# Self-attention of layer 3 on Trainium2: one unrolled block, three score buffers, whole outputs ahead of the transposes

## The chip, the cores and the metric

The kernel is one program on one core of a Trainium2 chip. The metric is the device time of one execution in microseconds (us). The engines are TensorE (PE, its weight loads PEld), VectorE (DVE), ScalarE (ACT), GpSimd (POOL) and SyncE (SP), whose queue issues the DMAs.

## The reference

A four-layer network on x of shape (2, 1024, 256). Each layer adds a gated attention and a gated feed-forward part. Layer 3's attention begins with this self-attention (a1, 16 heads of width 32), followed by an MLP, a cross-attention to 64 keys with the same widths (a2) and another MLP:

```
q = einsum('bsc,hcd->bhsd', xn, wq); k, v likewise
a = softmax(einsum('bhsd,bhtd->bhst', q, k) * D ** (-0.5), axis=-1)
a = a * (arange(t)[None, :] > arange(s)[:, None])      # a1 alone; after the softmax
o = einsum('bhst,bhtd->bhsd', a, v)
x_out = x + o @ li1_w + li1_b
h = gelu(_ln(x_out, ln3_g, ln3_b) @ li2_w + li2_b)
return x_out + h @ li3_w + li3_b
```

So the softmax runs over all 1024 keys, and the mask keeps only keys after the query: of the eight key chunks of 128, query tile `si` needs chunks `si` to 7 once the sums are known.

## The kernel before

The stages follow each other; each ends in a barrier. The change touches three.

**Projection** (`stage_self_project`, lines 2028 to 2186). Eight pairs of token tiles. Each pair's q and k are split into three bf16 parts and sent to DRAM (line 2070), its values too (line 2078). The first four pairs also send a second copy, into entry number 8, that nothing but a superfluous load reads. After the fourth pair SP waits for all sends and issues the 17 DMAs that load entry 0 (`load_entry`, lines 2015 to 2025); ScalarE may overwrite a buffer of parts only once its sends have landed.

**Self-attention** (`stage_self_attention`, lines 2196 to 2401). An entry is a batch and four heads, so 8 entries. An entry has 32 units: a unit is a query tile of 128 rows and one head. The tiles come in the order 0, 7, 1, 6, 2, 5, 3, 4, four heads each. A unit `v` goes through these steps:

- `scores(v)` (2292, PE): four bf16 matmuls of 512 columns into two PSUM banks. There are two such pairs of banks (0 to 3), so `scores(v)` waits for the exponential of unit v-2.
- the row maximum (2390, DVE), the exponential with its row sum (2373, ACT), the reciprocal of the sum (2397, DVE).
- the multiplication by the reciprocal, over the columns from `si * 128` on (2273, POOL, `tensor_tensor` with a broadcast operand), and the mask on the diagonal chunk (2276, POOL).
- `turn(v)` (2308, PE, five units later): 8 - si transposes, in one or two bankfuls (two where more than four chunks), banks 4 and 5 in turn; the even bankful is copied out by ACT (2359), the odd by DVE (2361).
- `output(w, q)` (2326, PE): w is a group of four units (a tile). From ten units later on, its matmuls of 32 columns (four heads at four column positions of the array) run in four visits q, one per unit, each with the chunks whose number has remainder q. Banks 6 and 7; ACT copies the result out (708 by `copy_bank`).

PE's queue has per unit: scores(v), turn(v-5), a visit of output. DVE's has maximum(v), its copy of unit v-5, reciprocal(v-1). ACT's has its copy of unit v-5, exponential(v), and every fourth unit the copy of an output. Four entries form the body of a hardware loop that runs twice; at its end everything drains, the semaphores are cleared, and the next body begins with no unit in flight.

**Cross-attention** (`stage_attention`, lines 336 to 677) serves l0a (width 64), l2a (16) and l3a (32), 16 heads each. In the wide form the output weights are folded with the values beforehand (`fold_v`, line 482, four of eight folds of a chunk), and each token tile needs eight matmuls of 256 columns (542). The narrow form makes the heads' outputs first (522, from a block `v_blk` with zeros), copies them with ACT (708) and multiplies by `wo` (533). Before a turn of the norm (222) PE waits in the narrow form for that copy:

```
                    if i >= TURN and (i - TURN) % 2 == 0:
                        if narrow:
                            pe.wait_ge(heads_stored, min(i - HEADS_OUT + 1, TILES))
```

Of the kernel before, what the change touches and what calls it, by code (L numbers as in the profile page):

```python
# [15 lines left out]
B = 2  # L16
# [319 lines left out]
def stage_attention(core, a, name, width, scale, plan, following, source, out_tile, gate, bias,  # L336
# [16 lines left out]
    narrow = width * 4 <= KEYS  # L353
# [1617 lines left out]
def self_attention_scratch(nc):  # L1971


    def dram(name, shape, dtype):
        return nc.dram_tensor(name, shape, dtype, kind="Internal").ap()


    parts = [[dram(f"l3_{kind}_part{m}", [ENTRIES + 1, P, TOK], BF16) for m in range(3)] for kind in ("q", "k")]
    values = dram("l3_values", [ENTRIES + 1, P, KC, P], F32)
    heads_out = dram("l3_heads_out", [ENTRIES, P, TOK], F32)  # L1980
    return parts, values, heads_out
# [46 lines left out]
def stage_self_project(core, a, x1, scratch, entry, plan):  # L2028
# [6 lines left out]
    with ExitStack() as ctx:  # L2035
# [21 lines left out]
        with nc.Block() as block:  # L2057
            @block.sync
            def _(sp):
                total = [0, 0]  # L2060
                for k in range(PAIRS):
                    b, p, at = k // (PAIRS // B), k % 2, (k % (PAIRS // B)) * PAIR
                    places = [(b * GROUPS, GROUPS)]
                    if b == 0:
                        places.append((ENTRIES, 1))
# [23 lines left out]
            def sent_before(k):  # L2089

                return sum(16 * 8 * (2 if q < PAIRS // B else 1) for q in range(k % 2, k, 2))
# [104 lines left out]
def stage_self_attention(core, scratch, entry, following):  # L2196
# [8 lines left out]
    BODY = 4  # L2205
    RING = 8
    TURN = 5
    STORE = TURN
# [17 lines left out]
    assert BANKFULS % 2 == 0  # L2226

    def groups_through(u):

        return sum(1 for g in groups if g[0] <= u)  # L2230

    with ExitStack() as ctx:
# [13 lines left out]
        with nc.Fori(0, ENTRIES // BODY) as jj:  # L2246
            sem, clear_semaphores = named_semaphores(nc, "l3s")
            scores_ready, measured, exped, inverted = sem("scores_ready"), sem("measured"), sem("exped"), sem("inverted")
            masked, turned, stored = sem("masked"), sem("turned"), [sem("stored0"), sem("stored1")]
            out_ready, out_stored = sem("out_ready"), sem("out_stored")  # L2250
            out_sent = [sem(f"out_sent{e}") for e in range(BODY)]

            with nc.Block() as block:
                @block.sync
                def _(sp):
                    load_entry(sp, scratch, entry, BODY * jj + 1, 1)
                    for e in range(BODY):

                        sp.wait_ge(out_ready, KC * (e + 1))
                        if e < BODY - 1:  # L2260
                            load_entry(sp, scratch, entry, BODY * jj + e + 2, e % 2)
                        sp.wait_ge(out_stored, KC * (e + 1))
                        sp.dma_start(out_scratch[bass.ds(BODY * jj + e, 1)].rearrange("a p n -> p (a n)"),
                                     heads_out[:, e % 2, :]).then_inc(out_sent[e], 16)
                    for e in range(BODY):
                        sp.wait_ge(out_sent[e], 16)

                @block.gpsimd
                def _(pool):
                    for v in range(BODY * UNITS):  # L2270
                        si = tile_of(v)
                        pool.wait_ge(inverted, v + 1)
                        nc.gpsimd.tensor_tensor(ex[v % RING][:, si * P:], ex[v % RING][:, si * P:],  # L2273
                                                sm[:, v % RING:v % RING + 1].to_broadcast([P, TOK - si * P]), ALU.mult)
                        pool.drain()
                        nc.gpsimd.affine_select(out=ex[v % RING][:, si * P:(si + 1) * P], in_=ex[v % RING][:, si * P:(si + 1) * P],
                                                compare_op=ALU.is_gt, fill=0.0, base=0, pattern=[[1, P]],
                                                channel_multiplier=-1).then_inc(masked, 1)
# [449 lines left out]
```

## Time and profile before

| | us |
|---|---|
| median of 3 runs (2547.37 to 2549.26) | 2548.7 |
| the profiled execution | 2524.31 |
| its span | 2522.6 |
| projection's last pair to self-attention's first matmul | 951 to 967.0 |
| self-attention, first body | 967.0 to 1225.9 |
| self-attention, second body, to its last DMA | 1225.9 to 1477.1 |
| first l3a fold to the next stage's first matmul | 1666.7 to 1831.6 |

Mean granted clock of PE over the span 0.902 of full speed. An engine's busy time is what its instructions take; back to back they can overlap by some 0.1 us, so starts are the better measure of pace.

### The profile page before, as it was taken

The numbers are of one execution on the slowest core, as the hardware profiler recorded it, in microseconds if no ns is written. First come the engines' busy times: TensorE is split into PE (matmuls) and PEld (weight loads), VectorE is DVE, ScalarE is ACT, GpSimd is POOL, SyncE is SP. The second block draws the span as 40 slices with busy tenths as digits, with TensorE's granted clock in tenths as the row PEclk, the third lists the DMA queues.
The fourth block names the chain that finished last, engine by engine and source line by source line (L and its number), as shares of the span: only waits on it lengthen the run. The fifth ranks groups of instructions, "written<-read, shape, count | busy, mean of one in ns | idle before, by whom it ended". The sixth has DMA issues, their size and how long they took to land. (4 is left out here: it accounts for less than half of the span.)

```text
span 2522.6 us, 36317 instructions
## 1 busy us (share of the span) xinstructions
PE 2047.2 (81%) x11904; PEld 1504.7 (60%) x11904; DVE 1367.6 (54%) x3511; ACT 929.6 (37%) x1859; POOL 710.5 (28%) x1199
## 2 busy tenths in 40 slices
PE   5983974467867677999799979969898589999991
PEld 4661863354444454555455558846687378888991
DVE  4871006535745765888688847757636432222332
ACT  4220321112324346888688843232232112222230
POOL 0223011030130125777577751102330230000005
PEclk9995995578979789999999989979999699999995
DMA  2004531000011286333333430110000525555684
GB/s 87 1 1 150 167 104 28 13 13 14 1 19 12 82 216 165 85 85 85 86 65 92 97 108 11 28 36 1 1 13 1 193 104 175 175 175 175 215 287 115
DMA packets 171504, 219.20 MB, mean 87 GB/s; under 512 B 39911, under 2 KB 133540, under 8 KB 165184
## 3 DMA queue, kind: packets, MB, share of 16 engines
q1 hardware_dynamic: 163344, 196.65, 26.7%
q0 software_dynamic: 7264, 20.31, 2.5%
q8 instruction: 88, 1.44, 0.2%
q14 instruction: 88, 0.72, 0.1%
q10 hardware_dynamic: 720, 0.07, 0.0%
HBM read 171.13 MB, written 46.14 MB: 86 GB/s over the span
## 5 line engine op out<-in xcount | busy, mean ns | idle before, releaser
L2390 DVE TENSOR_REDUCE l3s_mx<-banks 128x1 f32<-128x1024 f32 x256 | 313.1, 1223 | 96.7 <-PE banks L2292 93.8
L2292 PE MATMUL banks<-l_stack 128*128 128x512 bf16 x1024 | 268.1, 385 | 44.1 <-ACT xn_tokens L2373 21.0
L1012 PE MATMUL banks<-l3f_xrt,l3f_w 128*128 128x256 f32 (+1 forms) x1536 | 277.9, 342 | 2.7 <-issue 1.5
L1012 PEld LDWEIGHTS banks<-l3f_xrt,l3f_w 128*128 128x128 f32 x1536 | 249.6, 192 | 29.1 <-issue 3.3
L1302 DVE TENSOR_SCALAR l3f_sg<-banks 128x256 f32<-128x256 f32 (+1 forms) x192 | 72.0, 375 | 287.5 <-PE banks L1012 287.5
L2273 POOL TENSOR_TENSOR xn_tokens<-xn_tokens,l3s_sm 128x1024 f32<-128x1024 f32 (+3 forms) x128 | 201.6, 1575 | 50.3 <-DVE l3s_sm L2397 49.2
L222 PE MATMUL banks<-ident,xn_tokens 128*128 128x128 f32 x320 | 64.7, 338 | 166.8 <-DVE xn_tokens L211 148.0
L2292 PEld LDWEIGHTS banks<-l_stack 128*128 128x128 bf16 x1024 | 80.8, 98 | 163.3 <-ACT xn_tokens L2373 52.6
L2373 ACT ACTIVATE xn_tokens<-banks,l3s_mx 128x1024 f32<-128x1024 f32 x128 | 142.7, 1115 | 46.2 <-DVE l3s_mx L2390 45.1
L222 PEld LDWEIGHTS banks<-ident,xn_tokens 128*128 128x128 f32 x320 | 46.6, 172 | 188.4 <-DVE xn_tokens L211 133.0
L2373 ACT ACTIVATE x_features<-banks,l3s_mx 128x1024 f32<-128x1024 f32 x128 | 143.0, 1117 | 27.9 <-DVE l3s_mx L2390 27.6
L1077 ACT ACTIVATE l3f_sg<-l3f_sg 128x256 f32<-128x256 f32 (+1 forms) x192 | 72.2, 376 | 208.9 <-DVE l3f_sg L1302 208.9
L1025 PE MATMUL banks<-l3f_w,l3f_ht 128*128 128x256 f32 x624 | 138.5, 379 | 0.0
L930 POOL DMA_DIRECT2D l3f_results<-l3f_yt x24 | 15.8, 658 | 410.7 <-ACT l3f_yt L708 410.7
L1025 PEld LDWEIGHTS banks<-l3f_w,l3f_ht 128*128 128x128 f32 x624 | 116.8, 190 | 14.9
L2537 PE MATMUL banks<-x_features,weights 128*128 128x256 f32 x512 | 117.5, 390 | 4.3 <-ACT x_features L235 2.4
L2308 PEld LDWEIGHTS banks<-ident,xn_tokens 128*128 128x128 f32 x832 | 96.5, 140 | 29.1 <-issue 10.2
L2550 PE MATMUL banks<-weights,l3m_ht 128*128 128x256 f32 x512 | 113.2, 379 | 0.4 <-DVE l_x L2605 0.4
L2308 PE MATMUL banks<-ident,xn_tokens 128*128 128x128 f32 x832 | 112.6, 273 | 0.5 <-ACT l3s_pt L2359 0.5
L2537 PEld LDWEIGHTS banks<-x_features,weights 128*128 128x128 f32 x512 | 100.1, 196 | 19.5 <-issue 3.8
L2273 POOL TENSOR_TENSOR x_features<-x_features,l3s_sm 128x128 f32<-128x128 f32 (+3 forms) x128 | 92.4, 722 | 65.6 <-DVE l3s_sm L2397 64.6
L2359 ACT ACTIVATE l3s_pt<-banks 128x384 f32<-128x384 f32 (+2 forms) x192 | 97.0, 505 | 24.2 <-PE banks L2326 18.5
(532 smaller groups left out, 3925.4 us busy)
## 6 DMA issues: line engine op xcount, KB each, us to landing
l3f_w<-in_L_ffn_gate_up_w_dram SPq DMA_DIRECT2D x24, 2048.0 KB, 7.6
l3f_w<-in_L_ffn_down_w_dram SPq DMA_DIRECT2D x24, 1024.0 KB, 6.0
l_stack<-l_q_part SPq DMA_DIRECT2D x72, 256.0 KB, 6.0
l_stack<-l_k_part SPq DMA_DIRECT2D x72, 256.0 KB, 11.4
l0f_w<-in_L_ffn_W_dram SPq DMA_DIRECT2D x16, 1024.0 KB, 5.8
l_q_part<-l_stack SPq DMA_DIRECT2D x24, 256.0 KB, 3.0
l_k_part<-l_stack SPq DMA_DIRECT2D x24, 256.0 KB, 3.7
l3f_rows<-l3f_zero SPq DMA_DIRECT2D x13, 384.0 KB, 4.1
```

Of the source, the lines that this page charges most:

```text
L222: last = nc.tensor.transpose(ps[:, bank, c * PAIR + u * P:c * PAIR + (u + 1) * P], src(2 * j + u)[:, c * P:(c + 1) * P], core["ident"][:, :])
L1012: last = nc.tensor.matmul(ps[:, f % 4, h * PAIR:h * PAIR + size], w1_sb[:, p, dc, h * FF + f * P:h * FF + (f + 1) * P], xrt[:, p, dc, 0:si ...
L1025: last = nc.tensor.matmul(ps[:, 4 + p, u * D:(u + 1) * D], ht[:, p, f, u * P:(u + 1) * P], w2_sb[:, p, f, :], start=(f == 0), stop=(f == F ...
L1077: nc.scalar.activation(sg[:, f % 4, 0:size], sg[:, f % 4, 0:size], ACT.Silu).then_inc(silued, 1)
L2273: nc.gpsimd.tensor_tensor(ex[v % RING][:, si * P:], ex[v % RING][:, si * P:], sm[:, v % RING:v % RING + 1].to_broadcast([P, TOK - si * P]) ...
L2292: last = nc.tensor.matmul(ps[:, 2 * (v % 2) + h, :], stack[p][0][s][:, r, si * P:(si + 1) * P], stack[p][1][s][:, r, h * 512:(h + 1) * 512 ...
L2308: last = nc.tensor.transpose(ps[:, 4 + n % 2, c * P:(c + 1) * P], ex[v % RING][:, (si + c0 + c) * P:(si + c0 + c + 1) * P], core["ident"][ ...
L2359: last = op.activation(dst, src, ACT.Copy)
L2373: nc.scalar.activation(ex[v % RING][:, :], ps[:, 2 * (v % 2):2 * (v % 2) + 2, :].rearrange("p a n -> p (a n)"), ACT.Exp, bias=mx[:, v % RI ...
L2390: nc.vector.tensor_reduce(mx[:, v % RING:v % RING + 1], ps[:, 2 * (v % 2):2 * (v % 2) + 2, :].rearrange("p a n -> p (a n)"), AX_X, ALU.max ...
L2537: last = nc.tensor.matmul(ps[:, n % 4, 0:PAIR], w2[:, dc, f * P:(f + 1) * P], core["xt"][:, dc, PAIR * j:PAIR * (j + 1)], start=(dc == 0), ...
L2550: last = nc.tensor.matmul(ps[:, 4 + k % ring, u * D:(u + 1) * D], ht[:, k % 2, f, u * P:(u + 1) * P], w3[:, f, :], start=(f == 0), stop=(f ...
```

## The change

One entry after the other in a single block of 8 entries, unrolled (before, a loop of two bodies). The score buffers are three pairs of banks (0 to 5). Transposes and outputs share banks 6 and 7 in the order of their use (`uses`), and whoever empties a bank is given by the parity of the use: ACT even, DVE odd. By that rule the outputs fall to DVE (w = 0 to 63, all odd), and of an entry's 48 bankfuls of transposes 28 go to ACT and 20 to DVE.

```diff
-    narrow = width * 4 <= KEYS
+    narrow = width * 2 <= KEYS
...
-    parts = [[dram(f"l3_{kind}_part{m}", [ENTRIES + 1, P, TOK], BF16) for m in range(3)] for kind in ("q", "k")]
+    parts = [[dram(f"l3_{kind}_part{m}", [ENTRIES, P, TOK], BF16) for m in range(3)] for kind in ("q", "k")]
...
-                    if b == 0:
-                        places.append((ENTRIES, 1))
...
+    SCORES = 3
+
+    uses, last_turn = {}, {}
+    for v in range(ENTRIES * UNITS + OUT):
+        if v >= OUT and (v - OUT) % R == 0:
+            uses["out", (v - OUT) // R] = len(uses)
+        if TURN <= v < ENTRIES * UNITS + TURN:
+            for g, group in enumerate(groups):
+                if group[0] == (v - TURN) % UNITS:
+                    uses["turn", (v - TURN) // UNITS, g] = len(uses)
+                    last_turn[(v - TURN) // R] = uses["turn", (v - TURN) // UNITS, g]
...
-        with nc.Fori(0, ENTRIES // BODY) as jj:
...
-                        nc.gpsimd.tensor_tensor(ex[v % RING][:, si * P:], ex[v % RING][:, si * P:],
-                                                sm[:, v % RING:v % RING + 1].to_broadcast([P, TOK - si * P]), ALU.mult)
+                    nc.gpsimd.tensor_scalar(ex[v % RING][:, si * P:], ex[v % RING][:, si * P:],
+                                            sm[:, v % RING:v % RING + 1], None, ALU.mult)
...
+                    if v >= SCORES:
+                        pe.wait_ge(exped, v - SCORES + 1)
...
+                def output(w):
+                    e, si = w // KC, ORDER[w % KC]
+                    n = uses["out", w]
+                    for side in range(2):
+                        pe.wait_ge(stored[side], stored_through(side, max(last_turn[w], n - 2 if side == n % 2 else 0)))
+                    for c in range(si, KC):
+                        for r in range(R):
+                            last = nc.tensor.matmul(ps[r * W:(r + 1) * W, 6 + n % 2, 0:P],
+                                                    values[:, e % 2, c, r * W:(r + 1) * W],
+                                                    pt[:, w % 2, r, c - si, :], start=(c == si),
+                                                    stop=(c == KC - 1))
+                    last.then_inc(out_ready, 1)
...
+                    if v < ENTRIES * UNITS:
+                        scores(v)
+                    if v >= OUT and (v - OUT) % R == 0:
+                        output((v - OUT) // R)
+                    if TURN <= v < ENTRIES * UNITS + TURN:
+                        turn(v - TURN)
...
+            @block.scalar
+            def _(act):
+                for v in range(ENTRIES * UNITS + OUT + 1):
+                    store_output(act, nc.scalar, v, 0)
+                    if v >= TURN:
+                        store_turned(act, nc.scalar, v - TURN, 0)
...
+            @block.vector
+            def _(dve):
+                for v in range(ENTRIES * UNITS + OUT + 1):
+                    store_output(dve, nc.vector, v - 1, 1)
+                    if v >= TURN + 1:
+                        store_turned(dve, nc.vector, v - TURN - 1, 1)
+                    if v < ENTRIES * UNITS:
+                        dve.wait_ge(scores_ready, v + 1)
...
```

`stored_through(side, n)` counts the uses of a side up to n. So DVE's queue has output(v-1) and its copy of unit v-6 ahead of maximum(v), then reciprocal(v-1). `narrow` now holds for width 32 too, so l3a takes the narrow form.

## Rows read from the trace of the kernel before

**Rows 1.** The page: busy time of each engine, share of the span, instructions.

```profile
PE 2047.2 (81%) x11904; PEld 1504.7 (60%) x11904; DVE 1367.6 (54%) x3511; ACT 929.6 (37%) x1859; POOL 710.5 (28%) x1199
```

**Rows 2.** Windows, self-attention: length, then busy us (instructions) by engine, clock.

```profile
967.00:1225.90 258.90, 237.58 (x2240) 134.59 (x2241) 207.67 (x352) 200.61 (x386) 182.90 (x256) 0.99 0.37 87
...
1046.80:1107.60 60.80, 58.59 (x560) 33.41 (x558) 51.57 (x89) 49.68 (x96) 45.47 (x64) 1.00 0.38 88
```

**Rows 3.** Timeline of SP's queue: the load that follows each entry's last output.

```profile
1046.86 3.64 SPq L2023 DMA_DIRECT2D l_stack<-l_q_part  x8
...
1108.02 4.19 SPq L2023 DMA_DIRECT2D l_stack<-l_q_part  x8
```

**Rows 4.** Timeline of PE: start us, modelled us, line, instructions in a run.

```profile
1057.69 0.93 PE L2308 MATMUL banks<-ident,xn_tokens 128*128 128x128 f32 x7
1058.45 1.03 PE L2292 MATMUL banks<-l_stack 128*128 128x512 bf16 x4
...
1080.30 0.64 PE L2326 MATMUL banks<-l3s_pt,l_values_in 128*32 128x128 f32 x16
...
1101.87 1.04 PE L2292 MATMUL banks<-l_stack 128*128 128x512 bf16 x4
1102.75 1.04 PE L2308 MATMUL banks<-ident,xn_tokens 128*128 128x128 f32 x8
1103.71 0.43 PE L2326 MATMUL banks<-l3s_pt,l_values_in 128*32 128x128 f32 x8
1104.07 1.04 PE L2292 MATMUL banks<-l_stack 128*128 128x512 bf16 x4
```

**Rows 5.** Waits, 1010 to 1190 us: total us, times, longest.

```profile
PE banks L2292 <- ACT xn_tokens L2373: 5.8, 15, 0.6
```

**Rows 6.** Timeline of PE: the first scores of the second loop body.

```profile
1225.90 3.59 PE L2292 MATMUL banks<-l_stack 128*128 128x512 bf16 x8 [8.15 <-issue]
```

**Rows 7.** Groups by shape, 1010 to 1190 us.

```profile
L2390 DVE TENSOR_REDUCE l3s_mx<-banks 128x1 f32<-128x1024 f32 x95 | 116.2, 1223 | 26.5 <-PE banks L2292 25.2
...
L2373 ACT ACTIVATE xn_tokens<-banks,l3s_mx 128x1024 f32<-128x1024 f32 x48 | 53.5, 1115 | 15.2 <-DVE l3s_mx L2390 14.8
...
L2273 POOL TENSOR_TENSOR xn_tokens<-xn_tokens,l3s_sm 128x1024 f32<-128x1024 f32 x12 | 22.7, 1895 | 0.2
...
L2361 DVE COPY l3s_pt<-banks 128x384 f32<-128x384 f32 x29 | 15.9, 548 | 0.6 <-PE banks L2326 0.6
...
L2397 DVE RECIPROCAL l3s_sm<-l3s_sm 128x1 f32<-128x1 f32 x94 | 14.3, 153 | 0.0
...
L2273 POOL TENSOR_TENSOR x_features<-x_features,l3s_sm 128x128 f32<-128x128 f32 x12 | 4.8, 401 | 8.7 <-DVE l3s_sm L2397 8.5
...
L2361 DVE COPY l3s_pt<-banks 128x128 f32<-128x128 f32 x6 | 1.7, 280 | 0.0
```

**Rows 8.** Timeline of the projection stage: SP's queue and ScalarE.

```profile
906.70 2.17 SPq L2070 DMA_DIRECT2D l_q_part<-l_stack  x3
...
914.27 3.68 SPq L2023 DMA_DIRECT2D l_stack<-l_q_part  x8
...
942.92 1.09 ACT L2139 ACTIVATE l_stack<-banks 128x512 bf16<-128x512 f32 x2 [9.00 <-DMA l_values<-l3p_vs]
```

**Rows 9.** Windows of line 482 alone, folds of layer 3's cross-attention.

```profile
1670.00:1682.00 12.00, 11.44 (x53) 9.63 (x52) 1.00 0.01 1
```

**Rows 10.** Timeline of PE in layer 3's cross-attention (l3a).

```profile
1734.56 3.62 PE L542 MATMUL banks<-l3a_fold_v,l3a_pt 128*128 128x256 f32 x16
```

**Rows 11.** Timeline of PE in layer 2's cross-attention (l2a), the narrow form.

```profile
680.77 0.64 PE L522 MATMUL banks<-l2a_pt,l2a_v_blk 128*32 128x128 f32 x16
681.34 1.13 PE L533 MATMUL banks<-l2a_wo,l2a_heads 128*128 128x256 f32 x4
...
685.13 0.66 PE L222 MATMUL banks<-ident,xn_tokens 128*128 128x128 f32 x4 [2.66 <-ACT l2a_heads L708]
...
701.25 4.83 PE L499 MATMUL banks<-l2a_fold_q,x_features 128*128 128x512 f32 x8
```

More of the change, by code:

```diff
@@ L2089, in sent_before @@
             def sent_before(k):
-                return sum(16 * 8 * (2 if q < PAIRS // B else 1) for q in range(k % 2, k, 2))
+                return sum(16 * 8 for q in range(k % 2, k, 2))
             @block.gpsimd
@@ L2349, in store_turned @@
                     for g, (u, c0, size) in enumerate(groups):
[L2350 to L2351 removed]
+                        if u != v % UNITS:
                             continue
[L2353 to L2357 removed]
@@ L2399, in stage_self_attention @@
-            clear_semaphores()
-        nc.sync.wait_ge(loaded[0], 16 * LOADS * (ENTRIES // 2 + 1))
-        nc.all_engine_barrier()
+                        n = uses["turn", e, g]
+                        if n >= 2:
+                            pe.wait_ge(stored[n % 2], stored_through(n % 2, n - 2))
+                        for c in range(size):
+                            last = nc.tensor.transpose(ps[:, 6 + n % 2, c * P:(c + 1) * P],
+                                                       ex[v % RING][:, (si + c0 + c) * P:(si + c0 + c + 1) * P],
+                                                       core["ident"][:, :])
@@ new lines, in _ @@
+                for v in range(ENTRIES * UNITS + OUT):
+                    if v < ENTRIES * UNITS and v % UNITS == 0:
+                        e = v // UNITS
+                        pe.wait_ge(loaded[e % 2], 16 * LOADS * (e // 2 + 1))
+                    if v < ENTRIES * UNITS:
[4 more added lines that the diff above has]
+                        turn(v - TURN)
@@ new lines, in store_turned @@
+            def store_turned(eng, op, v, side):
+                if v >= ENTRIES * UNITS:
+                    return
+                e, w = v // UNITS, v // R
+                for g, (u, c0, size) in enumerate(groups):
+                    if u != v % UNITS or uses["turn", e, g] % 2 != side:
+                        continue
+                    n = BANKFULS * e + g
+                    eng.wait_ge(turned, n + 1)
+                    if w >= 2:
+                        eng.wait_ge(out_ready, w - 1)
+                    dst = pt[:, w % 2, v % R, c0:c0 + size, :].rearrange("p c n -> p (c n)")
+                    src = ps[:, 6 + side, 0:size * P]
+                    if side == 0:
+                        last = op.activation(dst, src, ACT.Copy)
+                    else:
+                        last = op.tensor_copy(dst, src)
+                    last.then_inc(stored[side], 1)
@@ new lines, in store_output @@
+            def store_output(eng, op, v, side):
+                if not OUT <= v < ENTRIES * UNITS + OUT or (v - OUT) % R != 0:
+                    return
+                w = (v - OUT) // R
+                e, si = w // KC, ORDER[w % KC]
+                if uses["out", w] % 2 != side:
+                    return
+                eng.wait_ge(out_ready, w + 1)
+                if e >= 2:
+                    eng.wait_ge(out_sent[e % 2], 16 * (e // 2))
+                dst, src = heads_out[:, e % 2, si * P:(si + 1) * P], ps[:, 6 + side, 0:P]
+                last = op.activation(dst, src, ACT.Copy) if side == 0 else op.tensor_copy(dst, src)
+                last.then_inc(stored[side], 1)
@@ L2404, in self_out_weights @@
+        clear_semaphores()
 def self_out_weights(a):
```

201 lines of the change are left out of this document (62 added, 139 removed).

## The prediction

> **What bounds the kernel now.** The page first: PE is busy 81% of the span, DVE 54% [rows 1], an average over stages; the change lies in three of them, so I read those. The windows of self-attention come next: its first body takes 258.9 us, and in a steady stretch of 60.8 us PE is busy 58.59, DVE 51.57, ACT 49.68, POOL 45.47, at granted clock 1.00 [rows 2]. SP's queue gives the exact pace: the load behind an entry's last output starts at 1046.86 and at 1108.02, so **an entry takes 61.16 us** (the next ones 61.1 too) [rows 3]. Eight would take 489; the stage takes 510 because of its loop.
>
> Then PE's timeline, for what a unit costs PE by starts. Scores: 0.88 (1101.87 to 1102.75). A transpose: 0.109 (seven in 0.76). Eight of them before an output: 0.96, so up to 0.09 more at that change. An output visit of 8 records (one chunk, four heads) 0.36 (1103.71 to 1104.07); 16 records take 0.64 modelled where 8 take 0.43: 0.21 a chunk and 0.15 for the visit itself [rows 4]. An entry has 32 units, 4 x 36 = 144 transposes, 36 chunks and, by the remainders q, 4+1+4+2+4+3+4+4 = 26 visits. PE's own time is 32 x 0.88 + 144 x 0.109 + 36 x 0.21 + 26 x 0.23 (0.15 and 0.08 of the change) = 28.2 + 15.7 + 7.6 + 6.0 = 57.5 us. Measured 61.1: **3.6 us an entry are waits**. The list of waits has PE idle before scores for the exponential 5.8 us in 180 [rows 5], 2.0 an entry; the rest is gaps too short to be listed. So PE is the bound, with two score buffers as the second.
>
> **The parts.**
>
> *The loop.* The second body's first scores start at 1225.90 after 8.15 us idle [rows 6]; fill and drain around it cost too. All of it: 258.9 - 4 x 61.1 = **14.5 us** [rows 2, 3]. Unrolled, the join goes: minus 14.5. Only an instruction stream twice as long stands against that; it is fetched in either form, and I cost it at nothing.
>
> *Outputs whole.* 26 visits become 8: 18 x 0.23 = 4.1 us of PE an entry (18 x 0.15 = 2.7 if the change between shapes costs nothing). Chunks and matmuls stay. PE's own time becomes 53.4.
>
> *Three score buffers.* Scores wait for the exponential of v-3. The 3.6 us of waits can go, but they can't become a gain to the full, since other waits come up.
>
> *One pair of banks for transposes and outputs.* All outputs are DVE's, and it takes them behind the maximum and the reciprocal. After an output of tiles 7, 6, 5 or 4 come units with two bankfuls; the first goes to ACT's bank, the second needs the bank of the output. DVE has it free, counted from the end of scores(v), after the maximum 1.22, a reciprocal 0.15, the copy of 128 columns 0.28 [rows 7] and 0.15 that I assume for the hand-over: about 1.8. PE gets there after the output (0.36 to 1.0) and up to four transposes (0.44): 0.8 to 1.5. So stalls of 0.3 to 1.0, four an entry: **+2.4 us**.
>
> *DVE a turn later.* Its order becomes maximum(v), reciprocal(v-1), copy of v-5. Before, the copy lay between the maximum and the reciprocal, which covered the exponential of v-1 (1.12 [rows 7] and the read of its sum). Queued behind the reciprocal are now the copy, and behind that PE's next second bankful. DVE's work per entry is 51.6 us busy [rows 2]; four fewer copies (0.28 for one chunk, 0.55 for three) and eight outputs of 0.28 leave it at about 52, by starts (0.1 overlap each) about 50. In the tiles with two bankfuls a unit costs it 1.12 + 0.1 + 0.45 to 0.6 = 1.7 to 1.8 by starts, as much as PE's 0.88 + 0.87. There the two engines are even, and losses of handshake stay: I take 0.8 us an entry (0 to 3.2: sixteen units by 0.2).
>
> *GpSimd.* 1024 columns take 1895 ns, 128 take 401 [rows 7]: 1.67 ns a column. A per-partition scalar on a wide tile is not in the trace. Below, it saves nothing, since the list of waits has no wait of PE for POOL; above, see the rivals. I take 0: five units of lag cover it, and POOL has 15 us of slack an entry [rows 2]. If it were slower, `turn` would be late next.
>
> Sum for an entry: 53.4 + 2.4 + 0.8 = **56.6**, 4.5 less than 61.1; eight entries: **minus 36**. Ends: 53.4 (minus 62) and 61.1 (nothing).
>
> *Projection.* The second copies are 8 of 16 DMAs in each of four pairs. In three pairs they end long before the pair (15 us) does, and cost nothing. In the fourth SP issues six from 906.70, 3.6 us, and two of the values', 1.1, before the load of entry 0 can start at 914.27. That load fills the DMA engines, the next sends land late, and ACT waits 9.00 us at 942.92 for them [rows 8]; DVE and PE wait on ACT, to the end of the stage. 4.7 us earlier in, as much off that wait: **minus 4.5** (0 to 6).
>
> *Cross-attention l3a in narrow form.* Setup: 53 records are 26.5 folds in 12 us [rows 9], 0.45 each; 16 go, minus 7.2, and half of the first block's masking, minus 0.8. New ahead of the loop: two matmuls of 512 columns for the values (2 x 0.86 by the pace of the scores), their masking (0.7 as a 512-column copy) and hand-overs: plus 3. Net minus 5. Per tile: 8 matmuls of 256 columns take 3.62 modelled [rows 10], some 3.45 by starts, and so do the scores, 4 of 512. In their place heads and `wo`. l2a's heads, 16 records at 32 columns, take 0.57 [rows 11], against 1.75 for 16 records of 128 columns one after the other [rows 4]: four lie side by side. At 64 columns two fit: 0.14 + 0.87 = 1.0 (0.57 to 1.9). `wo` is half of the old product, 1.7, plus 0.1. So 2.8, and 0.1 for the change of shape: 0.55 less a tile. But before each norm turn PE waits for the heads' copy. In l2a it idles 2.66 and goes on at 685.13; 3.45 + 0.96 + 0.57 lie before 681.34, so that is 8.8 us after the scores began [rows 11]. l3a's PE arrives at 3.45 + 0.96 + 2.8 = 7.2, the copy of twice the columns ends at 9.0: 1.8 us idle, then 0.43 of norm. Before, such a tile took 3.45 + 0.87 + 3.45 + 0.43 = 8.2: plus 1.2. Five such turns, plus 6; eleven or so others at minus 0.55, minus 5, and a drain one turn longer, plus 3. Stage: minus 5 + 6 - 5 + 3 = minus 1; with what the clock may take (below) I book **plus 1** (-6 to +14).
>
> Of the clock: after the idle in l2a, the scores at 701.25 took 4.83 modelled us [rows 11], as many columns at the full clock 3.62 [rows 10], that is, part of them ran at 1.2 GHz instead of 2.4. The Trainium skill, TensorE: Matmul & The Clock Gate, section "A second HAM failure mode: psum-queue depth-cycling", says that short idles between groups of matmuls while cycling through PSUM banks are enough to make the clock fall and rise. By that rule self-attention, which cycles through banks all the time, should swing, and it is granted 1.00 [rows 2]: the measurement decides there.
>
> Total: -14.5 - 36 - 4.5 + 1 = -54. The profiled execution took 2524.31, so it would be 2470; it lay 24.4 below the median of the runs shown, and against that the **forecast is 2548.7 - 54 = 2495 us**.
>
> **The rivals.**
> - *DVE ties PE* (23%). The second bankful of a unit needs DVE's copy of the unit before, so PE can't run ahead however many score buffers there are, and the third does not do what it says. For it: 16 units an entry with two bankfuls, each 0.2 later. Against: by starts DVE has 10 us of slack an entry. Price: 56.6 + 2.9 = 59.5 an entry, minus 13; total minus 31: 2518.
> - *PE at its floor* (17%). The stalls fall where PE is ahead and cost nothing: 53.4 to 54.5 an entry, minus 57; total minus 75: 2474.
> - *The clock falls in l3a* (5%). PE idles 1.8 us ahead of five turns and again in the drain; at 1.2 GHz scores take 1.2 more in each as at 701.25, and heads and `wo` after the drain's idles twice their 2.8. Five by 1.2 and three by 2.8 are plus 14: 2509. That is the page's rule taken to this stage.
> - *GpSimd becomes the bound* (5%, the side slower than before). Place: the multiplication by a per-partition scalar. An entry has 18432 columns; at 1.67 ns 31 us, and 15 for the rest of POOL with 6 of gaps. It decides from 63 us an entry, or 2.3 ns a column. At twice today's 1.67: 21 + 62 = 83, eight times 22 more, less 18 gained elsewhere: 2707. Against: it reads one wide operand where `tensor_tensor` reads two. The Trainium skill, GPSIMD Engine Reference, section 3.1, gives 1.8 cycles an element as the best of a one-input loop and 2.6 for two inputs; no run here shows the first, and the second disagrees with rows 7 (1.67 ns are 2.0 cycles at the page's 1.2 GHz).
> - *Nothing gained beyond the join* (3%): new stalls eat the visits saved, l3a costs what the rest gives: within 0.2%.
>
> **How the numbers follow.** The forecast's own case (2480 to 2508) has 47%. Faster by over 0.2% (5 us, about what a measurement of this kernel can tell): all but the last two cases, 0.92; same 0.03; slower 0.05. The range takes in the floor's upper part and most of the DVE case: 2467 to 2528; it leaves out the GpSimd case and the ends of both.
>
> **What would show it.** The stage from first scores to last output near 455 us, one entry per 56.6 by SP's loads; no idle of 8 us in its middle; 8 output runs an entry; waits of the transposes (2308's line) for DVE near 2.4 us an entry; hardly any of scores for the exponential. ACT's wait near 942.92 at about 4.5. GpSimd's rows at or under 1895 ns. l3a: 16 folds fewer, heads of about 1.0, `wo` of 1.8, idle before norm turns near 1.8. It would be wrong if entries stay near 60, if the transposes wait for POOL, or if l3a's loop grows by more than 10.

## The result, and the profile of the changed kernel

The changed kernel takes **2583.3 us** (median of 4 runs, 2580.0 to 2586.0) where the kernel before takes 2548.0 on the same chip (2546.3 to 2549.3): ratio 1.0147, interval 1.0131 to 1.0163. That is 35 us slower; forecast were 54 us faster, and a range that ends at 2528. The profiled execution took 2580.03, its span 2578.4 us.

The page first, the busy time of each engine, and two of its groups, both of GpSimd's multiplication.

```profile
PE 2019.7 (78%) x11996; PEld 1498.2 (58%) x11996; DVE 1370.9 (53%) x3538; ACT 925.8 (36%) x1826; POOL 854.6 (33%) x1202
...
L2282 POOL TENSOR_SCALAR xn_tokens<-xn_tokens,l3s_sm 128x1024 f32<-128x1024 f32 (+3 forms) x128 | 302.5, 2363 | 15.1 <-DVE l3s_sm L2403 15.1
...
L2282 POOL TENSOR_SCALAR x_features<-x_features,l3s_sm 128x128 f32<-128x128 f32 (+3 forms) x128 | 138.6, 1083 | 0.1
```

Against [rows 1] PE, DVE and ACT hardly differ; POOL has 144 us more to do. Its column of idle says what that means: it waited 15.1 us for a row sum, once, at the start, and never again. An engine that waits for nobody is the one that others wait for. The windows of one steady entry and of the stage, against [rows 2]:

```profile
1043.70:1112.10 68.40, 57.34 (x560) 34.89 (x560) 52.56 (x93) 49.32 (x92) 63.84 (x65) 1.00 0.33 78
964.00:1518.60 554.60, 463.29 (x4480) 281.11 (x4480) 421.34 (x736) 396.23 (x737) 511.38 (x512) 0.99 0.30 69
```

POOL (the last of the five busy times) is busy 63.84 of 68.40 us, and the rest are its own short gaps. SP's queue gives the entry, as in [rows 3]:

```profile
1043.64 4.59 SPq L2023 DMA_DIRECT2D l_stack<-l_q_part  x8
...
1112.10 3.65 SPq L2023 DMA_DIRECT2D l_stack<-l_q_part  x8
...
1180.27 3.64 SPq L2023 DMA_DIRECT2D l_stack<-l_q_part  x8
```

**68.3 us an entry**, where 61.1 were and 56.6 were forecast. The groups by shape, 1010 to 1190 us, give the cause; the same instructions of [rows 7] took 1895 ns for 1024 columns and 401 for 128:

```profile
L2282 POOL TENSOR_SCALAR xn_tokens<-xn_tokens,l3s_sm 128x1024 f32<-128x1024 f32 x12 | 34.1, 2843 | 0.0
...
L2285 POOL TENSOR_SCALAR_AFFINE_SELECT x_features<-x_features 128x128 f32<-128x128 f32 x43 | 12.6, 293 | 6.0 <-issue 0.4
...
L2282 POOL TENSOR_SCALAR x_features<-x_features,l3s_sm 128x128 f32<-128x128 f32 x12 | 7.2, 603 | 0.0
```

(2843 - 603) / 896 columns is **2.50 ns a column**, where `tensor_tensor` took 1.67, and 0.28 us are left for the instruction itself (0.19 before). An entry's 18432 columns and 32 instructions are 46.1 + 9.1 = 55.2 us, the 32 selections 9.4, the gaps ahead of them 4.4: 69, within 1 us of the entry measured. The waits of 1010 to 1190 us (total, times, longest) name POOL, which in [rows 5] stood nowhere:

```profile
PE banks L2313 <- POOL xn_tokens L2285: 22.0, 23, 1.7
PE banks L2325 <- DVE l3s_pt L2359: 3.5, 7, 0.7
PE banks L2313 <- POOL x_features L2285: 2.3, 6, 0.4
```

Last the ends of the stages in PE's timeline: last output of self-attention and start of l3a in the kernel before, then in the changed kernel first scores, last output, start of l3a and start of the stage behind it; and ScalarE's wait in the projection, against [rows 8]:

```profile
1475.57 1.08 PE L2326 MATMUL banks<-l3s_pt,l_values_in 128*32 128x128 f32 x32 [0.26 <-issue]
...
1660.87 1.94 PE L462 MATMUL banks<-ident,weights 128*128 128x128 f32 x8 [1.97 <-PEq L44]
```

```profile
964.09 7.43 PE L2297 MATMUL banks<-l_stack 128*128 128x512 bf16 x20 [11.99 <-PEq L44]
...
1516.70 1.08 PE L2325 MATMUL banks<-l3s_pt,l_values_in 128*32 128x128 f32 x32 [0.69 <-ACT l3s_pt L2357]
...
1699.61 1.94 PE L462 MATMUL banks<-ident,weights 128*128 128x128 f32 x8 [1.96 <-PEq L44]
...
1864.81 15.54 PE L2541 MATMUL banks<-x_features,weights 128*128 128x256 f32 x64 [1.97 <-PEq L44]
```

```profile
940.06 1.08 ACT L2137 ACTIVATE l_stack<-banks 128x512 bf16<-128x512 f32 x2 [6.02 <-DMA l_values<-l3p_vs]
```

Self-attention begins at 964.09 (967.00 before: 2.9 earlier) and its last output starts 552.6 us later, where before it was 508.6: plus 44.0. The MLP behind it takes 182.9 against 185.3, l3a (1699.61 to 1864.81) 165.2 against 170.7. In all -2.9 + 44.0 - 2.4 - 5.5 = **+33 of the 35 us**. The experts' stage behind (layer 3's feed-forward) took 713.6 us in this trace and 691.0 in that of before (an execution of 2524.31); the medians, taken on one chip, leave hardly room for a difference there, and the experiments below are compared either with before on their own chip or stage by stage up to the experts.

### The profile page after: what moved, and what is told of

It is laid out like the page before. It is cut to its first block and busy times, and to the rows that moved or that the text cites. A ratio compares the mean times of both kernels' runs of the same rounds, so it can differ in the third digit from the quotient of the medians.

```text
span 2578.4 us, 36316 instructions
## 1 busy us (share of the span) xinstructions
PE 2019.7 (78%) x11996; PEld 1498.2 (58%) x11996; DVE 1370.9 (53%) x3538; ACT 925.8 (36%) x1826; POOL 854.6 (33%) x1202
## 5 line engine op out<-in xcount | busy, mean ns | idle before, releaser
L2282 POOL TENSOR_SCALAR xn_tokens<-xn_tokens,l3s_sm 128x1024 f32<-128x1024 f32 (+3 forms) x128 | 302.5, 2363 | 15.1 <-DVE l3s_sm L2403 15.1
L222 PE MATMUL banks<-ident,xn_tokens 128*128 128x128 f32 x320 | 65.0, 339 | 173.0 <-DVE xn_tokens L211 147.4
L2313 PE MATMUL banks<-ident,xn_tokens 128*128 128x128 f32 x832 | 125.9, 282 | 68.1 <-POOL xn_tokens L2285 59.9
L2313 PEld LDWEIGHTS banks<-ident,xn_tokens 128*128 128x128 f32 x832 | 89.3, 140 | 123.9 <-POOL xn_tokens L2285 98.9
L222 PEld LDWEIGHTS banks<-ident,xn_tokens 128*128 128x128 f32 x320 | 46.1, 172 | 196.4 <-DVE xn_tokens L211 125.7
L930 POOL DMA_DIRECT2D l3f_results<-l3f_yt x24 | 15.7, 656 | 435.0 <-ACT l3f_yt L708 435.0
L2357 ACT ACTIVATE l3s_pt<-banks 128x384 f32<-128x384 f32 (+3 forms) x224 | 109.3, 488 | 114.2 <-PE banks L2313 113.6
L2297 PEld LDWEIGHTS banks<-l_stack 128*128 128x128 bf16 x1024 | 101.3, 99 | 81.9 <-issue 16.4
L2282 POOL TENSOR_SCALAR x_features<-x_features,l3s_sm 128x128 f32<-128x128 f32 (+3 forms) x128 | 138.6, 1083 | 0.1
L2359 DVE COPY l3s_pt<-banks 128x384 f32<-128x384 f32 (+3 forms) x160 | 88.1, 551 | 54.4 <-PE banks L2313 53.3
```

The costliest lines, as they stand in the source:

```text
L222: last = nc.tensor.transpose(ps[:, bank, c * PAIR + u * P:c * PAIR + (u + 1) * P], src(2 * j + u)[:, c * P:(c + 1) * P], core["ident"][:, :])
L2282: nc.gpsimd.tensor_scalar(ex[v % RING][:, si * P:], ex[v % RING][:, si * P:], sm[:, v % RING:v % RING + 1], None, ALU.mult)
L2297: last = nc.tensor.matmul(ps[:, 2 * (v % SCORES) + h, :], stack[p][0][s][:, r, si * P:(si + 1) * P], stack[p][1][s][:, r, h * 512:(h + 1) ...
L2313: last = nc.tensor.transpose(ps[:, 6 + n % 2, c * P:(c + 1) * P], ex[v % RING][:, (si + c0 + c) * P:(si + c0 + c + 1) * P], core["ident"][ ...
L2357: last = op.activation(dst, src, ACT.Copy)
L2359: last = op.tensor_copy(dst, src)
```

## The experiments

The theory after the result: GpSimd's `tensor_scalar` costs 2.50 ns a column and bounds the stage; the rest of the change is a gain. Rivals: the unrolled order with two shared banks made the stage slow and GpSimd only shows it; or the gain expected of the rest isn't there either.

### 1. The old multiplication in the changed kernel (e1_tensor_tensor)

```diff
-nc.gpsimd.tensor_scalar(ex..., ex..., sm[:, v % RING:v % RING + 1], None, ALU.mult)
+nc.gpsimd.tensor_tensor(ex..., ex..., sm[:, v % RING:v % RING + 1].to_broadcast([P, TOK - si * P]), ALU.mult)
```

> The changed kernel with GpSimd's multiplication in the old form (tensor_tensor with a broadcast operand). Theory, GpSimd is the bound: its rows return to 1895 ns at 1024 columns, an entry falls from 68.2 us to about 56.6, eight of them 93 less, total near 2490. Rival, the two shared banks and VectorE's late emptying hold the stage nearly as much: an entry stays at 60 or more, total 2518 or more, and transposes then wait for VectorE by over 4 us an entry.

**2488.6 us where before takes 2520.2**: ratio 0.9873 (0.9854 to 0.9892). The ratios 1.0147 and 0.9873 differ by 2.7%, some 69 us, and that is GpSimd's line (by the traces its stage takes 487.1 us in place of 552.6, 65.5 less); the rows of 1024 columns are back at 1893 ns. But the rest gains 31.5 us and not 54. The total near 2490 that the first theory named was met by luck: it counted from before's 2548, and on this chip before takes 2520. SP's loads:

```profile
1093.85 3.65 SPq L2023 DMA_DIRECT2D l_stack<-l_q_part  x8
...
1335.48 3.81 SPq L2023 DMA_DIRECT2D l_stack<-l_q_part  x8
```

Four entries in 241.63 us: **60.4 an entry**, 0.7 under before and not 4.5, as the rival had it (60 or more). PE's timeline shows where the time is, around an output of tile 7:

```profile
1104.98 0.60 PE L2313 MATMUL banks<-ident,xn_tokens 128*128 128x128 f32 x4
1105.92 0.55 PE L2313 MATMUL banks<-ident,xn_tokens 128*128 128x128 f32 x3 [0.34 <-ACT l3s_pt L2357]
...
1108.04 0.43 PE L2325 MATMUL banks<-l3s_pt,l_values_in 128*32 128x128 f32 x8 [0.71 <-DVE l3s_pt L2359]
1108.39 0.66 PE L2313 MATMUL banks<-ident,xn_tokens 128*128 128x128 f32 x4
1109.34 0.55 PE L2313 MATMUL banks<-ident,xn_tokens 128*128 128x128 f32 x3 [0.29 <-DVE weights L2374]
```

Three waits belong to one output: 0.34 ahead of it, 0.71 for the bank that it shares with a bankful not yet copied, 0.29 for the copy of the output itself. I had booked only the last, at 2.4 us an entry. Over the entry from 1214.74 it takes 0.5 (the rival expected over 4), the first 0.9, and the wait of outputs for VectorE's copy, booked at nothing, 2.7. Summed by starts over one entry, each step to the start of the next less the idle shown in brackets (before: 1108.02 to 1169.11; this kernel: 1214.74 to 1274.86):

| us an entry | forecast took, before | trace, before | forecast, after | trace, this kernel |
|---|---|---|---|---|
| scores | 28.2 | 28.1 | 28.2 | 27.4 (28.9) |
| transposes | 15.7 | 18.9 | 15.7 | 19.7 (18.2) |
| outputs | 13.6 | 12.0 | 9.5 | 9.0 |
| idle listed | 3.6 | 2.1 | 3.2 | 4.1 |
| sum | 61.1 | 61.1 | 56.6 | 60.1 |

In this trace 8 of an entry's 128 records of scores are missing, and their time stands under transposes. How much that is, two traces of one kernel show, those of experiment 10: 27.4 and 19.5 us with 120 records, 29.0 and 18.0 with 128. The numbers in brackets are this kernel's with 1.5 us put back; experiment 8, at the same pace with all 128 records, reads 28.9 and 18.2. The transposes are the row that matters: 144 x 0.109 leaves out 3.2 us in before and 2.5 here, by the likeliest reading what each short run of them costs beside its columns, which no run took apart. In before the outputs, booked 1.6 too high, hid half of it: of the 3.6 us that I called waits only 2.1 were. Those did go, since nothing of scores for the exponential is listed here; 4.1 of waits for banks came in their place.

### 2. The new multiplication in the kernel before

```diff
-nc.gpsimd.tensor_tensor(ex..., ex..., sm[...].to_broadcast([P, TOK - si * P]), ALU.mult)
+nc.gpsimd.tensor_scalar(ex..., ex..., sm[...], None, ALU.mult)
```

> The kernel before with only GpSimd's multiplication in the new form. Theory, GpSimd is the bound: 2.5 ns a column make GpSimd 68 us an entry whatever the order of the rest, so an entry takes 68 instead of 61.1: plus 56 us, total near 2604. Rival, the long instruction is hidden by five units of lag, and it is the new order that exposes it: total within 10 us of 2548.

2583.2 against 2520.2: ratio **1.0244** (1.0227 to 1.0261), 63 us. Entries go to 68.3 (1124.49 to 1192.75), the same as in the changed kernel, whatever the order of the work:

```profile
1124.49 4.34 SPq L2023 DMA_DIRECT2D l_stack<-l_q_part  x8
...
1192.75 3.66 SPq L2023 DMA_DIRECT2D l_stack<-l_q_part  x8
```

```profile
L2273 POOL TENSOR_SCALAR xn_tokens<-xn_tokens,l3s_sm 128x1024 f32<-128x1024 f32 x9 | 25.6, 2844 | 0.0
```

Eight entries by 7.2 us are 58. Most of the other 5 lie where a body fills: from the load at its start to the next, 968.98 to 1056.27 and 1253.80 to 1346.40, it takes 9.4 us more than in before (968.92 to 1046.86, 1222.54 to 1305.76), 2.2 above the 7.2, twice. The one line alone makes either kernel slow.

### 3. An immediate in place of the pointer

```diff
-nc.gpsimd.tensor_scalar(ex..., ex..., sm[:, v % RING:v % RING + 1], None, ALU.mult)
+nc.gpsimd.tensor_scalar(ex..., ex..., 0.001, None, ALU.mult)
```

> The changed kernel with GpSimd's multiplication by an immediate (0.001) in place of the per-partition scalar: the division by the row sums is left out and all weights are scaled by a constant, the shape and count of the instructions stay. If the pointer to a per-partition scalar is what costs 2.50 ns a column, the immediate runs at 1.67 ns a column or less: 1024 columns take 1.9 us or less, an entry falls from 68.4 us to about 60.5, and the run ends some 60 us below the changed kernel, near 2490 us where before takes 2520. If tensor_scalar itself runs at 3 cycles of 1.2 GHz a column on this engine, the 1024 columns stay at 2.84 us, the entries at 68 us and the run near 2550.

This kernel leaves out the division by the row sums. It ran once: 2534.5 us, where before takes 2522.1. The groups by shape, 1050 to 1430 us:

```profile
L2282 POOL TENSOR_SCALAR xn_tokens<-xn_tokens 128x1024 f32<-128x1024 f32 x21 | 58.1, 2769 | 0.0
...
L2282 POOL TENSOR_SCALAR x_features<-x_features 128x128 f32<-128x128 f32 x21 | 11.1, 529 | 0.0
```

(2769 - 529) / 896 is 2.50 ns a column again. The per-partition pointer costs 74 ns an instruction and nothing a column: it is `tensor_scalar` itself that goes at this pace here, and the second theory holds for the columns. Its entries of 68 us and total near 2550 came out lower, since I had not expected the 74 ns: entries by SP's loads are 65.6 (1106.23 to 1368.43 for four), 2.7 fewer, of which 32 x 0.074 = 2.4 are the instructions.

### 4. Two score buffers

```diff
-    SCORES = 3
+    SCORES = 2
```

on the kernel of experiment 1.

> The first experiment with two score buffers instead of three. If the third buffer carries a part of the gain, an entry grows by the 2 to 3.6 us of waits that the kernel before had: plus 16 to 29 us on the first experiment. Rival, VectorE's emptying ties TensorE so closely that the third buffer is never used: within 5 us of the first experiment.

2540.4 against 2520.2: ratio 1.0081 (1.0062 to 1.0100), **52 us more than with three**. Both numbers that I gave were too small.

```profile
1108.30 3.64 SPq L2023 DMA_DIRECT2D l_stack<-l_q_part  x8
...
1174.35 4.28 SPq L2023 DMA_DIRECT2D l_stack<-l_q_part  x8
```

```profile
POOL x_features L2282 <- DVE l3s_sm L2403: 35.7, 36, 2.1
DVE l3s_mx L2398 <- PE banks L2297: 35.3, 74, 1.1
...
PE banks L2297 <- ACT xn_tokens L2387: 19.6, 41, 0.8
```

An entry takes 66.05. POOL waits for row sums, VectorE for scores (35.7 and 35.3 us in 240), and PE before scores for the exponential: 6.2 us over the entry from 1108.30, where with three buffers none is listed and in before 2.1. So the third buffer is worth 5.6 us an entry in this order, and the new order with its shared banks costs about 5 by itself. The likely mechanism, argued and not shown: PE, held for a bank, comes late with scores, and with two buffers nothing is in hand. The two parts belong together, and what the forecast counted as two gains is one that pays for the other.

### 5. l3a in its wide form

```diff
-    narrow = width * 2 <= KEYS
+    narrow = width * 4 <= KEYS
```

on the kernel of experiment 1.

> The first experiment with layer 3's cross-attention in the wide form of before. From the traces of before and after that stage takes 170.7 and 165.2 us, so this should be 5.5 us slower than the first experiment (3 to 8). Rival, the stage's gain is given back by the next one's start: within 2 us.

2497.3: ratio 0.9905 (0.9889 to 0.9922), **8.6 us more**, just over the 3 to 8 expected, and the traces give l3a 173.3 us in place of 165.0. The narrow form is worth 5.5 (changed against before) to 8.6 us.

### 6. The projection's second copies sent again

```diff
                     places = [(b * GROUPS, GROUPS)]
+                    if b == 0:
+                        places.append((ENTRIES, 1))
```

with the scratch and the counts as before, on the kernel of experiment 1.

> The kernel of e1_tensor_tensor, with the projection's second copies of entry 0 sent again (8 of 16 DMAs in four pairs). The forecast's step says 4.5 us slower than e1 (0 to 6); the two profiled executions of before and after differ by 2.9 at the start of the stage. If SP's queue ahead of entry 0's load is not what ends ScalarE's wait, within 1 us of e1.

2521.1 where before takes 2544.7 on that chip: ratio 0.9905 (0.9890 to 0.9920). Against experiment 1's ratio that would be 8 us, but chips differ behind self-attention; the traces up to there are cleaner. The load of entry 0 starts at 914.36 (910.53 in experiment 1), the longest of ScalarE's waits is 8.1 (5.3), self-attention begins at 965.84 (962.78), 3.1 us later. But 0.9 of it was there before the stage: the projection's first matmul starts at 841.35 and 840.42. From that matmul on, entry 0's load comes 73.0 to 73.1 us later in all three traces with the second copies (this one, before, experiment 2) and 70.0 to 70.1 later in the others, and self-attention begins 124.5 to 126.2 us later in the three and 121.8 to 123.4 in the eleven traces without them: **2.9 us** by the means, the load's 2.9 to 3.0. From its first scores to its last output the stage takes 486.7 and 487.1, the same.

```profile
914.36 3.66 SPq L2023 DMA_DIRECT2D l_stack<-l_q_part  x8
...
965.84 5.67 PE L2299 MATMUL banks<-l_stack 128*128 128x512 bf16 x16 [11.66 <-PEq L44]
```

```profile
ACT l_stack L2139 <- DMA l_values<-l3p_vs: 9.5, 2, 8.1
```

### 7. VectorE's copies at their old place (e6_vector_early)

```diff
-                    store_output(dve, nc.vector, v - 1, 1)
-                    if v >= TURN + 1:
-                        store_turned(dve, nc.vector, v - TURN - 1, 1)
...
+                    store_output(dve, nc.vector, v, 1)
+                    if v >= TURN:
+                        store_turned(dve, nc.vector, v - TURN, 1)
```

ahead of the reciprocal, on the kernel of experiment 1.

> The kernel of e1_tensor_tensor, with VectorE's copies of turned tiles and of outputs back behind the maximum of the same turn, as in the kernel before. If the later turn was needed, VectorE now waits for transposes that stand behind scores and an output in TensorE's queue, its reciprocals and next maximum come late, and entries go from 60.5 us to 61 to 62: 4 to 12 us slower than e1 (2493 to 2501 where before takes 2520). If instead the copy ahead of the maximum is what holds maximum, exponential and scores up, entries fall to 59 to 60 us: 4 to 12 us faster than e1. If VectorE has slack at both places, within 3 us of e1.

2484.1 against 2522.1: ratio **0.9846** (0.9829 to 0.9862). The interval touches that of experiment 1; the traces settle it: 59.1 us an entry (four in 236.41), 1.3 fewer, 480.1 for the stage where 487.1 were. The same output as above:

```profile
1106.88 0.43 PE L2325 MATMUL banks<-l3s_pt,l_values_in 128*32 128x128 f32 x8 [0.45 <-DVE l3s_pt L2359]
...
1108.18 0.55 PE L2313 MATMUL banks<-ident,xn_tokens 128*128 128x128 f32 x3 [0.29 <-DVE weights L2374]
```

0.45 in place of 0.71 for the bank. "A turn later" was a loss: over an entry these waits fall from 2.7 us to 1.7, and whatever VectorE's early copy delays in its own queue costs less than its late one costs PE.

### 8. Only VectorE's copy of an output earlier

```diff
-                    store_output(dve, nc.vector, v - 1, 1)
...
+                    store_output(dve, nc.vector, v, 1)
```

> The kernel of e1_tensor_tensor, with only VectorE's copy of an output (half of the 64) moved from ahead of the next turn's maximum to behind its own turn's maximum; turned tiles are still emptied a turn later. If the waits for banks end the time (0.29 us behind an output before the transposes that need its bank), 32 of these go, some 5 to 9 us faster than e1. If the entry is set by the chain of maximum, exponential and scores, the reciprocal comes a little later and the run stays within 3 us of e1.

2488.7: ratio 0.9868 (0.9850 to 0.9887), no difference from experiment 1 that can be told; 60.1 us an entry. All the outputs are VectorE's, not half of them as I wrote there, and moving these copies alone gains at most 0.3 an entry: the copies of turned tiles are what most of experiment 7's gain comes from.

### 9. Outputs behind the transposes

```diff
-                    if v >= OUT and (v - OUT) % R == 0:
-                        output((v - OUT) // R)
                     if TURN <= v < ENTRIES * UNITS + TURN:
                         turn(v - TURN)
+                    if v >= OUT and (v - OUT) % R == 0:
+                        output((v - OUT) // R)
```

with banks and copies numbered in that order, on the kernel of experiment 1.

> The kernel of e1_tensor_tensor, with outputs issued behind the transposes of their turn, banks numbered in that order. If issuing them ahead matters, each of the 64 outputs now waits for the copy of a bankful turned just before it, 0.5 to 1 us in place of the 0.6 to 0.73 us seen now for the copy of the last one: up to 1 us each, and 8 to 40 us over the stage. If the output pays one copy of a bank wherever it stands, because outputs share the two banks with the transposes, the run is within 5 us of e1.

2510.3 against 2522.1: ratio 0.9956 (0.9939 to 0.9972), **some 21 us more**; four entries take 250.83, 62.7 each.

```profile
1111.64 0.96 PE L2313 MATMUL banks<-ident,xn_tokens 128*128 128x128 f32 x7 [0.70 <-DVE l3s_pt L2359]
1113.43 0.43 PE L2325 MATMUL banks<-l3s_pt,l_values_in 128*32 128x128 f32 x8 [0.83 <-DVE l3s_pt L2359]
```

Transposes and output now wait, 0.70 and 0.83. So in this kernel, where they share banks, the output is better issued ahead.

### 10. ScalarE copies the outputs (e10_scalar_copies_outputs)

```diff
-                    store_output(act, nc.scalar, v, 0)
+                    for side in range(2):
+                        store_output(act, nc.scalar, v, side)
```

VectorE's call is gone, the bank's own semaphore is counted up as before, on the kernel of experiment 7.

> The kernel of e6_vector_early, with all outputs copied by ScalarE; until now all 64 fall to VectorE, 0.29 us each. If the shared pair of banks and VectorE's turn order set what is left above TensorE's own work (0.29 us of idle behind four outputs an entry, 2.3 us of VectorE's time an entry), entries fall from 59.7 to about 58.5 us: 6 to 12 us faster than e6, near 2475 where before takes 2520. If ScalarE's exponentials then come late (it waits for the output ahead of each one), the gain is eaten: within 3 us of e6 or slower.

2499.0 against 2544.7: ratio **0.9816** (0.9796 to 0.9837). Entries 58.6 us (four in 234.56). Run again beside the next experiment:

> The kernel of e10_scalar_copies_outputs once more, on the same chip as the run with copies chosen by place, as the measure for it: entries of 58.6 us, and 46 us less than before.

2478.9 against 2523.0, ratio 0.9826 (0.9812 to 0.9839), entries 58.6, 44 us less than before. Against experiment 7 that is 0.5 us an entry, 4 in all (5 to 8 by the ratios, taken on different chips), under the 6 to 12 expected. The wait of 0.29 behind an output is gone from the list; what is left at it:

```profile
1105.33 0.55 PE L2313 MATMUL banks<-ident,xn_tokens 128*128 128x128 f32 x3 [0.34 <-ACT l3s_pt L2357]
...
1107.19 0.43 PE L2325 MATMUL banks<-l3s_pt,l_values_in 128*32 128x128 f32 x8 [0.45 <-DVE l3s_pt L2359]
1107.55 1.20 PE L2313 MATMUL banks<-ident,xn_tokens 128*128 128x128 f32 x7
```

### 11. The engine of a copy by its place in the unit

```diff
-                    if u != v % UNITS or uses["turn", e, g] % 2 != side:
+                    bank = uses["turn", e, g] % 2
+                    pair = [q for q in range(BANKFULS) if groups[q][0] == u]
+                    if u != v % UNITS or (bank if len(pair) == 1 else pair.index(g)) != side:
```

on the kernel of experiment 10.

> The kernel of e10_scalar_copies_outputs, with the engine of a copy chosen by its place and no longer by its bank: where a unit has two bankfuls ScalarE copies the first and VectorE the second. An output then waits for a copy of ScalarE that runs during the maximum, not for one of VectorE behind it. If these waits (0.42 us, four an entry) and the 0.34 behind each change of parity are what is left, entries fall from 58.6 to 56.5 to 57.5 us: 9 to 17 us faster than e10. If the first bankful behind an output now waits for VectorE's copy of the second one before it, the wait only moves: within 4 us of e10.

2476.8 against 2523.0: ratio **0.9819** (0.9806 to 0.9832), entries 58.6: the same as experiment 10 within its interval. The wait only moved, as the second case has it:

```profile
1104.14 0.55 PE L2313 MATMUL banks<-ident,xn_tokens 128*128 128x128 f32 x3 [0.34 <-ACT l3s_pt L2359]
...
1105.94 0.43 PE L2325 MATMUL banks<-l3s_pt,l_values_in 128*32 128x128 f32 x8 [0.39 <-ACT l3s_pt L2359]
...
1107.12 0.55 PE L2313 MATMUL banks<-ident,xn_tokens 128*128 128x128 f32 x3 [0.16 <-ACT weights L2376]
```

Now ScalarE holds the output 0.39. Every one of these kernels with `tensor_tensor` in it but experiment 4's beats both kernels of the change; the best two are 1.8% under before.

## Why the prediction was wrong

**GpSimd: the step that failed.** I wrote "I take 0" for an operation that the trace of before doesn't show. It cost 2.50 ns a column where 1.67 were, and experiments 1 and 2 put 69 and 63 us on that line alone. The rival's own sum was sound: with the measured 2.50 it gives 21 + 46 = 67 an entry and, eight times 6 more less 18, some 2579; measured 2583. (The forecast with 68.3 in place of 56.6 comes to 2495 + 8 x 11.7 = 2589; the 6 between are l3a's, below.) What was wrong is its chance, 5%, its price at a doubling, and its threshold: 63 us or 2.3 ns is where the whole change becomes a loss, but by the same terms (21 beside the columns) GpSimd bounds the forecast's 56.6 from 1.93 ns a column on, 1.16 times the 1.67. The 15 us of slack were counted without its gaps and against the old, longer entry, and nothing in any row said that the unseen form could not be a sixth slower. I let "it reads one wide operand where `tensor_tensor` reads two" stand as a reason against, and the range left the case out. The Trainium skill, GPSIMD Engine Reference, section 3.1, points the same way: its best loop takes 1.8 cycles an element (one input, as I read it), and `tensor_tensor` with its two inputs 2.6. By that page the line would have become faster; at the page's 1.2 GHz the rows are 3.0 cycles for the one input and 2.0 for two. The order is the reverse, and the measurement decides.

**The steady entry.** Without GpSimd the entry is 60.4 (experiment 1), forecast 56.6. Two terms of the sum: the transposes, 15.7 booked and 18.9 in the same trace of before, which I could have found by summing one entry by starts as in the table of experiment 1; and the banks, 2.4 and 0.8 booked, 4.1 listed. Against the forecast's 56.6 experiment 1 has 2.5 more in transposes, 0.9 more in idle, 0.7 more in scores and 0.5 less in outputs. Outputs whole were worth 3.0 (4.1 forecast). What held is the rival "DVE ties PE" in its price, 59.5 an entry and 2518 in all: 0.9873 of 2548.7 is 2516. That the totals agree so well is luck: its entries are 0.9 us short (7 in all), and its l3a 7 too long. In its mechanism it held only half: it was the copy's place in VectorE's order (experiment 7 took 1.3 off) and its having every output (experiment 10 took 0.5 more), not VectorE's load. That the third buffer "does not do what it says" was wrong: experiment 4 puts 52 us on it.

**The loop.** Minus 14.5 forecast. Stage less eight entries: 508.6 - 8 x 61.1 = 19.8 before, 487.1 - 8 x 60.4 = 3.9 in experiment 1: minus 16. It held, and the longer stream of instructions shows no cost.

**The projection.** Minus 4.5 forecast, 2.9 measured (experiment 6), by the mechanism named: counted from the stage's first matmul, SP reached entry 0's load 2.9 to 3.0 earlier, and ScalarE's longest wait shrank from 9.0 and 8.1 to between 5.2 and 6.3. The size was off: I took the removed sends' 4.7 us of issuing as the shift.

**Layer 3's cross-attention.** Plus 1 forecast, minus 5.5 to 8.6 measured. Heads of 16 records take 1.03 by starts (1.0 forecast), `wo` 1.84 (1.8), idle before the norm's transposes 1.50 once and 1.28 four times (1.8). Scores stay at 3.60 modelled, where l2a's took 4.83 [rows 11]: the clock granted from 1733 to 1833 us is 1.00, so these idles did not bring it down. In the drain it did fall: the mean of the two levels, 1.2 and 2.4 GHz, is 0.78 of full speed from 1833.0 to 1864.8, where PE idles 2.78, 1.20 and 6.81 us at a time, and the heads take 1.97 modelled in place of 1.09. Before's drain has 0.88 (1797.5 to 1831.6). The tile's prices held. The lines of a steady tile, a norm turn, and last the heads and `wo` in the drain at the lower clock:

```profile
1758.27 3.60 PE L499 MATMUL banks<-l3a_fold_q,x_features 128*128 128x512 f32 x8
1761.70 1.04 PE L509 MATMUL banks<-ident,l3a_ex 128*128 128x128 f32 x8
1762.66 1.09 PE L522 MATMUL banks<-l3a_pt,l3a_v_blk 128*64 128x128 f32 x16
1763.69 1.99 PE L533 MATMUL banks<-weights,l3a_heads 128*128 128x256 f32 x8
1767.18 0.65 PE L222 MATMUL banks<-ident,xn_tokens 128*128 128x128 f32 x4 [1.50 <-ACT l3a_heads L708]
...
1846.99 1.97 PE L522 MATMUL banks<-l3a_pt,l3a_v_blk 128*64 128x128 f32 x16 [1.20 <-ACT x_features L235]
1848.89 2.90 PE L533 MATMUL banks<-weights,l3a_heads 128*128 128x256 f32 x8
```

Taken apart by PE's starts, changed kernel against before, then experiment 1 against experiment 5: the setup (to the first scores) gives -5.7 and -7.0 where -5 was forecast; from the first to the last scores -2.9 and -2.0, forecast +1; from there to the next stage +3.1 and +0.7, forecast +3 and 2 for the clock. So setup and drain were near, and the loop and the clock were priced too high. In the loop, a steady tile gains 0.51 and a norm turn loses 1.00, as forecast within 0.2; the rest lies in its first turns, up to the first `wo`, where one run of before's scores also took 5.24 modelled us in place of 3.60.

Added up for experiment 1: -16 - 8 x 0.7 - 2.9 - 5.7, and -1.8 in the MLP between (183.5 for 185.3, its cause not followed) are -32, measured -31.5. With GpSimd's 8 x 7.9 = +63 and a longer fill and drain (552.6 - 8 x 68.3 = 6.2 in place of 3.9): +33, measured +35.

**What stays open.** Why `tensor_scalar` is slower a column than `tensor_tensor` on this engine no run shows. Of the 58.6 us that the best kernels take an entry 2.6 are idle listed by PE's timeline and 56 its own steps, so most of what is left would have to come from the steps themselves, such as fewer or wider transposes; that was not tried.

## What to carry to other kernels

Where a change swaps an instruction for one that the trace doesn't have, divide the engine's slack at the pace that you forecast, gaps counted, by the work at stake: a factor of 1.16 was all that lay between "free" and "the bound" here, and no argument about operands is a measurement. Sum one whole period by starts before calling a rest "waits": of the 3.6 us an entry that I took for waits 2.1 were, and others came in their place. And where two parts of a change share a resource (outputs in the transposes' banks, a third buffer in the banks so freed), price them as one, since here one part costs what the other gives.

## What the runs showed of the hardware

- GpSimd, f32, 128 partitions: `tensor_scalar` 2.50 ns a column and 0.28 us an instruction by a per-partition pointer, 2.50 and 0.21 by an immediate; `tensor_tensor` with the same column broadcast 1.67 ns and 0.19 us. The one with fewer operands is the slower.
- The experts' stage, the same code everywhere, took 691.0 and 713.6 us in two traces of this case, and before took 2520 to 2548 us by chip, more than most parts of the change are worth. Only comparisons on one chip, or of a stage's own length, carry here; and a stage's start on the span's clock moves by some us with what lies before it (the projection's first matmul: 838.4 to 842.9 us in fourteen traces).
